# One pair deeper in the attention, and staged gate weights in the experts

## The chip, the cores and the metric

The kernel runs on one core of one Trainium2 chip. TensorE (PE) multiplies matrices, VectorE (DVE) and ScalarE (ACT) work element by element, GpSimd (Pool) does here mainly indirect transfers (gather and scatter of rows), and SyncE (SP) issues the other transfers. They run in parallel and wait for one another through semaphores. The metric is the device time of one execution in microseconds.

## The reference

Two layers over 16 sequences of 256 tokens with 128 features. Layer 0 is a recurrent mixer gated by an 8-expert network; the change doesn't touch it. Layer 1 is an attention of 16 heads gated by a network of 160 experts, of which each token uses 8:

```python
q = proj(wq, bq); k = proj(wk, bk); v = proj(wv, bv)          # 16 heads of 64
scores = jnp.einsum('bhqd,bhkd->bhqk', q, k) * scale
attn = jax.nn.softmax(scores, axis=-1)
ctx = jnp.einsum('bhqk,bhkd->bhqd', attn, v)
s = jnp.einsum('bsd,hd->bsh', ctx, wo) + bo
...
combine = combine.at[jnp.arange(T)[:, None], top_idx].set(top_w)   # 8 of 160 experts
h1 = jax.nn.silu(jnp.einsum('th,eih->eti', x, w_gate))             # 64 hidden each
routed = jnp.einsum('eti,ehi->th', h1 * combine.T[:, :, None], w_down)
shared = jax.nn.silu(x @ w_gate_shared.T) @ w_down_shared.T
x = x + s * silu(routed + shared)
```

## The kernel before, in words

Layer 1 comes in three stages: the attention of sequences 0 to 7, then the experts, then the attention of sequences 8 to 15. Beside the first half Pool scatters the tokens to the experts' slots in DRAM (`xs_dram`, 256 scatters of 128 rows, L555), and DVE works out the routing weights. Beside the second half Pool gathers the experts' rows (L567, 256 gathers), and DVE adds them up, weighted.

**The attention** goes by pairs of heads, 8 for each sequence, 64 for a half, numbered p. The steps of a pair are a chain over the engines: PE projects q and k (`qk_mm`, three passes each, high and low parts), ACT writes the high part and DVE the low part (`qk_out`, `qk_low`); PE makes the scores of both heads (`both_scores`, L1045) in `ps_s`, DVE takes the negated row maxima (L1734), ACT the exponentials with their sums (`exps`, L741, two for each head); PE turns the probabilities (`turn_probs`, L1058), ACT copies them (`probs_out`, L718), PE multiplies them with the values (`values`, L1078). Beside that DVE inverts and spreads the sums (`invert_sums`, `spread_sums`, L1699), PE turns them (`turn_rsums`, L1066), ACT copies them (`rsums_out`, L733), DVE normalises the context (`normalise`, L1706) and PE projects it (`project`, L1088). Each engine runs a fixed order written by hand, in which different steps belong to different pairs. A step that finds its semaphore too low stops all that stands behind it on its engine. For the scores of pair p, `attend` on PE waits until the exponentials of pair p-1 have read the banks (`exp_done`).

Pool's scatters are paced: every second one waits for `tr_done`, the count of turned heads, so that they spread over the half; each also waits until an earlier one has landed.

**The experts** run over 42 iterations (`NBODY`) of 1024 slots, in two halves h of four tiles of 128 slots. A tile belongs to one pair of experts (2 x 64 hidden columns make 128), whose number stands in a table (`pair_row`). For a half, PE turns the slots (`turn_slots`), ACT copies them (`xT_out`); PE multiplies them with the gate weights (`up1`): the slots are the stationary operand and the weights, at an address that PE reads from the table, are streamed. ACT applies SiLU (`silu`), PE turns the result (`turn_hidden`), DVE writes it masked by which expert of the pair owns the slot (`hidden_out`; `own_of` makes the mask), PE multiplies with the down weights (`down_1`), ACT or DVE copies the rows, and SP stores them. Pool has nothing to do in this stage.

## Time and profile before

| | |
|---|---|
| median of 3 runs | 1999.31 us (1998.68 to 2007.2) |
| the profiled execution's own time | 1999.14 us |
| its span | 1997.3 us |
| busy: PE, DVE, ACT, Pool | 1750.2, 1208.2, 971.0, 687.6 us |
| first half of the attention | 853.5 to 1282.1 us |
| experts | 1282.1 to 1512.5 us |
| shared expert | 1512.5 to 1547 us |
| second half of the attention | 1547 to 1995 us |

Times of the profile count from the start of the span. The stages' edges were set by hand: the first scores of each half, the first slots that PE turns (1282.10), and the shared expert's start. Names of tiles that share memory can stand for one another: `xn_buf` holds maxima and sums of the attention, and the slots and, in the changed kernel, the staged weights of the experts; `gate` is the gate weights.

### The profile page before, as it was taken

What the parts mean: (1) busy time and instruction counts of PE and PEld (TensorE: products, weight loads), DVE (VectorE), ACT (ScalarE), POOL (GpSimd) and SP (SyncE); (2) the same over time, 40 slices, a digit from 0 to 9 for tenths busy, and PEclk for the clock granted to TensorE, in tenths of its full rate; (3) what the DMA queues carried; (4) which work ended last, traced back from release to release, by engine and by line L of the source; (5) the groups of instructions that cost most, each with busy time, mean ns of one, the idle gap of its engine ahead of it and who ended that gap; (6) DMA issues with size and microseconds to landing.
All of it is one profiled execution on the core that took longest, in us unless ns stands there. A gap on an engine that the chain in (4) does not pass through costs nothing.

```text
span 1997.3 us, 47676 instructions
## 1 busy us (share of the span) xinstructions
PE 1750.2 (88%) x13222; PEld 1445.1 (72%) x13309; DVE 1208.2 (60%) x4593; ACT 971.0 (49%) x3034; POOL 687.6 (34%) x735
## 2 busy tenths in 40 slices
PE   5889999999999996787888888899997888777878
PEld 2557699999999776465666666699995666565656
DVE  4553445555555677866666766666663666666667
ACT  2311244444444224365666666655552666555656
POOL 0034412222222004255555555300003555555552
PEclk9988999999999998798999999999998899999999
DMA  9901101111110302111111111377672111111111
GB/s 355 373 21 34 35 24 37 37 37 37 37 37 26 87 0 99 78 34 42 65 39 66 41 64 39 111 197 197 197 198 74 36 45 38 41 42 42 44 42 30
DMA packets 153598, 153.77 MB, mean 77 GB/s; under 512 B 17027, under 2 KB 132294, under 8 KB 153286
## 3 DMA queue, kind: packets, MB, share of 16 engines
q1 hardware_dynamic: 130404, 104.23, 16.5%
q0 software_dynamic: 22272, 47.29, 7.8%
q10 hardware_dynamic: 866, 1.58, 0.2%
q8 instruction: 25, 0.41, 0.1%
q14 instruction: 31, 0.25, 0.0%
HBM read 71.10 MB, written 81.94 MB: 77 GB/s over the span
## 4 chain that ended last, share of the span: by engine, by line
PE 60%; DVE 14%; another core or an unknown queue 9%; issue 8%; ACT 7%; DVEq 1%; DMA 1%; ACTq 0%
PE ps_y L861 7%; ACT probs L741 5%; PE ps_up L1045 4%; PE ps_y L919 4%; PE ps_up L910 4%; PE ps_up L1140 4%; PE ps_t L1157 4%; PE ps_y L1058 3%; PE ps_rec L874 3%; PE ps_rec L876 3%; PE ps_t L879 3%; PE ps_t L877 3%; PE ps_rec L1015 3%; DVE xn_buf L1734 3%
## 5 line engine op out<-in xcount | busy, mean ns | idle before, releaser
L567 POOL DMA_INDIRECT rows_g<-ys_dram,slot x256 | 248.7, 971 | 446.7 <-DMA ys_dram<-slots_y 241.7
L741 ACT ACTIVATE probs<-ps_up,xn_buf 128x256 f32<-128x256 f32 x512 | 236.4, 477 | 191.0 <-DVE xn_buf L1734 166.1
L555 POOL DMA_INDIRECT xs_dram<-xn_buf,slot x256 | 247.3, 966 | 198.3 <-issue 89.8
L1734 DVE TENSOR_REDUCE xn_buf<-ps_up 128x2 f32<-128x512 f32 x256 | 166.9, 687 | 208.9 <-remote 123.6
L1058 PE MATMUL ps_y<-misc,probs 128*128 128x128 f32 x1024 | 171.6, 298 | 115.6 <-ACT probs L741 92.2
L1058 PEld LDWEIGHTS ps_y<-misc,probs 128*128 128x128 f32 x1024 | 117.2, 148 | 161.6 <-ACT probs L741 135.0
L861 PE MATMUL ps_y<-zeros 128*128 128x512 bf16 x660 | 193.8, 388 | 1.8 <-issue 0.2
L1354 DVE SCALAR_TENSOR_TENSOR mixn<-ps_rec,cols_sb,th_r 128x16 f32<-128x16 f32 x256 | 59.8, 233 | 217.7 <-ACT th_r L625 116.9
L525 POOL DMA_INDIRECT ys_dram<-slots_y,row_ids x80 | 78.1, 977 | 300.9 <-DVE slots_y L1484 240.3
L718 ACT COPY probsT<-ps_y 128x512 f32<-128x512 f32 x256 | 147.8, 598 | 32.9 <-remote 16.4
L1078 PE MATMUL ps_t<-probsT,v_sb 128*64 128x256 f32 x1024 | 143.1, 400 | 5.9 <-ACT probsT L718 3.3
L625 ACT ACTIVATE th_r<-ps_rec 128x16 f32<-128x16 f32 x256 | 46.7, 182 | 208.2 <-PE ps_rec L874 196.6
L1045 PE MATMUL ps_up<-kT,qT 64*128 64x256 f32 x1536 | 136.8, 314 | 0.3 <-issue 0.3
L1015 PE MATMUL ps_rec<-xr,w_high 128*128 128x256 f32 x528 | 123.8, 329 | 4.9 <-DVE xr L1669 3.5
L865 PEld LDWEIGHTS ps_rec<-gin,misc 128*128 128x128 f32 x514 | 98.5, 193 | 40.1 <-issue 6.9
L1045 PEld LDWEIGHTS ps_up<-kT,qT 64*128 64x128 f32 x1536 | 109.4, 203 | 19.7 <-issue 5.5
L1088 PE MATMUL ps_t<-aw,ctxT 128*128 128x128 f32 x512 | 94.6, 309 | 25.4 <-DVE ctxT L1706 16.6
L919 PE MATMUL ps_y<-w_sb,h_sb 128*128 128x128 f32 x640 | 110.5, 295 | 0.0
L644 ACT ACTIVATE h_sb<-ps_up,b_sb 128x256 f32<-128x256 f32 x160 | 75.9, 474 | 69.6 <-PE ps_y L919 63.3
L868 PEld LDWEIGHTS ps_t<-gin,misc 128*128 128x128 f32 x514 | 88.0, 193 | 28.9 <-issue 15.6
L910 PE MATMUL ps_up<-slots_xT,w_sb 128*128 128x256 f32 x320 | 108.5, 421 | 0.0
L627 ACT ACTIVATE th_zv<-ps_t 128x32 f32<-128x32 f32 x256 | 50.6, 198 | 116.7 <-PE ps_t L879 108.5
(250 smaller groups left out, 4364.6 us busy)
## 6 DMA issues: line engine op xcount, KB each, us to landing
xn_buf<-xs_dram SPq DMA_DIRECT2D x88, 256.0 KB, 2.8
xs_dram<-zeros SPq DMA_DIRECT2D x42, 512.0 KB, 5.7
ys_dram<-slots_y SPq DMA_DIRECT2D x84, 256.0 KB, 2.4
slots_x<-xs_dram SPq DMA_DIRECT2D x41, 130.0 KB
xs_dram<-zeros SPq DMA_DIRECT2D x10, 520.0 KB, 4.6
gate<-w_gate SPq DMA_DIRECT2D x1, 5120.0 KB, 15.9
down<-w_down SPq DMA_DIRECT2D x8, 640.0 KB
w_sb<-w POOLq DMA_DIRECT2D x16, 256.0 KB, 3.0
```

The lines of the kernel that those rows point to most:

```text
L555: nc.gpsimd.indirect_dma_start(xs_dram, bass.IndirectOffsetOnAxis(ap=slot[:, n, k:k + 1], axis=0), xn_tok[:, n, :], None).then_inc(scatter ...
L567: nc.gpsimd.indirect_dma_start(rows_g[:, i % 16, :], None, ys_dram, bass.IndirectOffsetOnAxis(ap=slot[:, i // TOPK1, i % TOPK1:i % TOPK1 + ...
L718: nc.scalar.copy(probsT[:, a, :, :].rearrange("p c t -> p (c t)"), ps_y[:, a, :]) \
L741: nc.scalar.activation(probs[:, a, i, :], ps_s[a][:, T * i:T * i + T], ACT.Exp, bias=negmax[:, a, i:i + 1], accum_out=sums[:, j % 4, i, a: ...
L861: nc.tensor.matmul(ps_y[:, 1, :], warm_b[:, 0:P], warm_b[:, 0:512], start=True, stop=True)
L910: nc.tensor.matmul(ps_up[j % 2][:, 0:256], w1_sb[:, wbuf, P * j:P * j + P], slots0_xT[:, :], start=True, stop=True).then_inc(up_ready, 1)
L919: last = nc.tensor.matmul(ps_y[:, 0, P * s:P * s + P], h_sb[:, j % 2, P * s:P * s + P], w2_sb[:, wbuf, j, :], start=(j == 0 and s == 0), s ...
L1015: last = nc.tensor.matmul(dst, left[a_], right[b_], start=(k == 0), stop=(k == 2))
L1045: last = nc.tensor.matmul(ps_s[a][:, T * i:T * i + T], qT[rows_a, j % 2, a_, P * i:P * i + P], kT[rows_a, j % 2, b_, :], start=(k == 0), s ...
L1058: last = nc.tensor.transpose(ps_y[:, a, T * kc + P * i:T * kc + P * i + P], probs[:, a, i, P * kc:P * kc + P], ident)
L1078: last = nc.tensor.matmul(ps_ctx[HD * a:HD * a + HD, 0:T], v_sb[:, j % 2, kc, HD * a:HD * a + HD], probsT[:, a, kc, :], start=(kc == 0), s ...
L1734: V.tensor_reduce(negmax[:, a, :], ps_s[a][:, :].rearrange("p (i t) -> p i t", i=2), AX_X, ALU.max, negate=True).then_inc(max_ready, 1)
```

## The change

**In the attention** PE, ACT and DVE turn, copy, invert and multiply for a pair one step older than before. PE's order in a pair p was: scores(p), project(p-2), value projection(p+1), values(p-1), turned sums(p-1), turned probabilities(p), query/key projection(p+2). It is now: scores(p), turned probabilities(p-1), value projection(p), turned sums(p-2), values(p-2), project(p-3), query/key projection(p+2). The turned sums have moved from the bank of the context to that of the value projection. The drain behind each half has more steps. Pool's scatters wait for the same counts shifted by two, while the turning comes one pair later.

**In the experts** Pool copies the gate weights of each tile, addressed by the table, to a staging buffer of two iterations (`staged`), and PE holds them as the stationary operand and streams the turned slots. The product then comes out turned, `turn_hidden` and its buffer go, and DVE masks the hidden in place in SBUF.

```diff
+        staged = xn_tok[:, 16:32, :].rearrange("p (u h s) d -> p u h (s d)", u=2, h=2)
...
-                        pool.wait_ge(tr_done, (n * TOPK1 + k) // 2 - 3)
+                        pool.wait_ge(tr_done, (n * TOPK1 + k) // 2 - 1)
...
+            def stage(it, h, u, waits=True):
+
+                pool.reg_load(pool_word[h], words[0:1, bass.ds(it * 2 + h, 1)])
+                if waits:
+                    pool.wait_ge(up1_done[h], it - 1)
+                for s in range(4):
+                    nc.gpsimd.tensor_copy(staged[:, u, h, P * s:P * s + P],
+                                          gate1[:, bass.ds(pair_of(pool, pool_word[h], s) * P, P)]) \
+                        .then_inc(staged_by_pool[h], 1)
+
+            for k in range(2):
+                pool.wait_ge(scattered[k], 16 * NT * TOPK1 // 2)
+            pool.wait_ge(gate_loaded, 16)
+            pool.wait_ge(table_loaded, 32)
+            for u in range(2):
+                for h in range(2):
+                    stage(u, h, u, False)
+            with pool.Fori(1, NBODY // 2) as i:
+                for u in range(2):
+                    for h in range(2):
+                        stage(i * 2 + u, h, u)
...
-                nc.scalar.copy(rsumsT[:, :], ps_ctx[:, T:2 * T]).then_inc(rsumsT_ready, 1)
+                nc.scalar.copy(rsumsT[:, :], ps_v[:, T:2 * T]).then_inc(rsumsT_ready, 1)
...
+                    if not (first and j < 2):
+                        rsums_out(p - 2, not (first and j == 2))
                     if not early:
-                        rsums_out(p - 1, not (first and j == 1))
-                    probs_out(p, 0, not early)
-                    probs_out(p, 1, not early)
-                    if j == PAIRS - 2:
+                        for a in range(2):
+                            probs_out(p - 1, a, not (first and j == 1))
...
+                    if not early:
+                        for a in range(2):
+                            turn_probs(p * 2 - 2 + a, p - 1, a, not (first and j == 1))
+                    v_mm_(b, j, p, x)
                     if not (first and j < 2):
-                        project(p - 2, (j - 2) % PAIRS, None if first else b)
-                    v_mm_(b + (j + 1) // PAIRS, (j + 1) % PAIRS, p + 1, x)
-                    if not early:
-                        values(p - 1, (j - 1) % PAIRS, not (first and j == 1))
-                        turn_rsums(p - 1)
-                    for a in range(2):
-                        turn_probs(p * 2 + a, p, a, not early)
+                        turn_rsums(p - 2)
+                        values(p - 2, (j - 2) % PAIRS, not (first and j == 2))
+                    if not (first and j < 3):
+                        project(p - 3, (j - 3) % PAIRS, None if first else b)
                     qk_mm(b + (j + 2) // PAIRS, (j + 2) % PAIRS, p + 2, x)
...
-            def up1(it, h):
-
-                pairs = pairs_of(next_word[h])
+                pe.reg_load(pe_word[h], words[0:1, bass.ds(it * 2 + h, 1)])
+
+            def up1(i, u, h):
+
+                it = i * 2 + u
                 pe.wait_ge(xT_ready[h], it + 1)
+                pe.wait_ge(staged_by_pool[h], 4 * it + 4)
                 for s in range(4):
-                    last = nc.tensor.matmul(ps_up[h][:, P * s:P * s + P], slots_xT[:, h, P * s:P * s + P],
-                                            gate1[:, bass.ds(pairs[s] * P, P)], start=True, stop=True)
+                    last = nc.tensor.matmul(ps_up[h][:, P * s:P * s + P], staged[:, u, h, P * s:P * s + P],
+                                            slots_xT[:, h, P * s:P * s + P], start=True, stop=True)
                 last.then_inc(up1_done[h], 1)
...
-            def turn_hidden(it, h):
-
-                pe.wait_ge(silu1_done[h], it + 1)
-                for s in range(4):
-                    last = nc.tensor.transpose(ps_y[:, h, P * s:P * s + P], hid[:, h, P * s:P * s + P], ident)
-                last.then_inc(h_turned[h], 1)
...
-            def down_1(it, h, reg):
-
-                pairs = pairs_of(reg)
+            def down_1(it, h):
+
                 pe.wait_ge(hT_ready[h], it + 1)
                 pe.wait_ge(y_out[h], it + 1)
                 for s in range(4):
-                    last = nc.tensor.matmul(ps_t[h][:, P * s:P * s + P], hidT[:, h, P * s:P * s + P],
-                                            down1[:, :, :].rearrange("p k n -> p (k n)")[:, bass.ds(pairs[s] * P, P)],
-                                            start=True, stop=True)
+                    last = nc.tensor.matmul(ps_t[h][:, P * s:P * s + P], hid[:, h, P * s:P * s + P],
+                                            down1[:, :, :].rearrange("p k n -> p (k n)")
+                                            [:, bass.ds(pair_of(pe, pe_word[h], s) * P, P)], start=True, stop=True)
                 last.then_inc(down1_done[h], 1)
...
             def expert_turn(i, u, rest=True):
 
                 it = i * 2 + u
-                if rest:
-                    up1(it, 0)
-                if rest:
-                    turn_hidden(it - 1, 1)
-                turn_slots(i, u + 1, 0)
-                if rest:
-                    down_1(it - 1, 0, last_word[0])
-                load_word(it + 1, 0)
-                up1(it, 1)
-                turn_hidden(it, 0)
-                turn_slots(i, u + 1, 1)
-                if rest:
-                    down_1(it - 1, 1, last_word[1])
-                load_word(it + 1, 1)
+                for h in range(2):
+                    if rest:
+                        down_1(it - 1, h)
+                        load_word(it, h)
+                    up1(i, u, h)
+                    turn_slots(i, u + 1, h)
...
-                project(p - 2, PAIRS - 2, None)
+                for a in range(2):
+                    turn_probs(2 * p - 2 + a, p - 1, a, True)
+                pe.wait_ge(v_ready, p)
+                turn_rsums(p - 2)
+                values(p - 2, PAIRS - 2, True)
+                project(p - 3, PAIRS - 3, None)
+                pe.wait_ge(normed, p - 1)
+                turn_rsums(p - 1)
                 if x == 0:
                     pe.wait_ge(qk_ready, p + 1)
                     turn_slots(0, 0, 0)
                 values(p - 1, PAIRS - 1, True)
-                turn_rsums(p - 1)
-                if x == 0:
-                    pe.wait_ge(gate_loaded, 16)
-                    pe.wait_ge(table_loaded, 32)
-                    for h in range(2):
-                        pe.reg_load(next_word[h], words[0:1, h:h + 1])
-                    up1(0, 0)
+                project(p - 2, PAIRS - 2, None)
                 project(p - 1, PAIRS - 1, None)
...
-                    if not (first and j < 2):
-                        normalise(p - 2)
-                    values_out(p, j, x, not (first and j < 2))
-                    if j == 2 and not first:
+                    if not (first and j < 3):
+                        normalise(p - 3, not (first and j == 3))
+                    if not early:
+                        values_out(p - 1, (j - 1) % PAIRS, not (first and j < 3))
+                    if j == 3 and not first:
...
-                    invert_sums(p, j)
+                    if not early:
+                        invert_sums(p - 1, j + 3, not (first and j == 1))
                     side_work(b, j, x, (2, 3))
-                    spread_sums(p, not early)
+                    if not early:
+                        spread_sums(p - 1, not (first and j == 1))
...
-                dve.wait_ge(h_turned[h], it + 1)
+                dve.wait_ge(silu1_done[h], it + 1)
                 dve.wait_ge(own_ready[h], it + 1)
-                V.tensor_tensor(hidT[:, h, :], ps_y[:, h, :], own[:, h, :], ALU.mult).then_inc(hT_ready[h], 1)
+                V.tensor_tensor(hid[:, h, :], hid[:, h, :], own[:, h, :], ALU.mult).then_inc(hT_ready[h], 1)
```

On PE, one pair of the attention before, from its scores (L1045) to the query/key projection (L1015); L1058 turns probabilities, L1088 projects, L1036 projects values, L1078 is the values, L1066 turns sums:

```order
L1045 MATMUL ps_up<-kT,qT 128x256 x12
L1088 MATMUL ps_t<-aw,ctxT 128x128 x2
L1036 MATMUL ps_rec<-aw,xb 128x128 x2
L1078 MATMUL ps_t<-probsT,v_sb 64x256 x4
L1066 MATMUL ps_t<-misc,top 128x128 x2
L1058 MATMUL ps_y<-misc,probs 128x128 x8
L1015 MATMUL ps_rec<-xr,w_high 128x256 x2
L1015 MATMUL ps_rec<-xr,w_low 128x256
L1015 MATMUL ps_rec<-xr,w_high 128x256 x2
L1015 MATMUL ps_rec<-xr,w_low 128x256
```

and the same stretch in the changed kernel (L1082 scores, L1095 probabilities, L1073 value projection, L1103 sums, L1115 values, L1125 project, L1052 query/key):

```order
L1082 MATMUL ps_up<-kT,qT 128x256 x12
L1095 MATMUL ps_y<-misc,probs 128x128 x8
L1073 MATMUL ps_rec<-aw,xb 128x128 x2
L1103 MATMUL ps_rec<-misc,top 128x128 x2
L1115 MATMUL ps_t<-probsT,v_sb 64x256 x4
L1125 MATMUL ps_t<-aw,ctxT 128x128 x2
L1052 MATMUL ps_rec<-xr,w_high 128x256 x2
L1052 MATMUL ps_rec<-xr,w_low 128x256
L1052 MATMUL ps_rec<-xr,w_high 128x256 x2
L1052 MATMUL ps_rec<-xr,w_low 128x256
```

Turning the probabilities has moved from in front of the query/key projection to right behind the scores. On ACT and DVE the rows of a pair read the same in both kernels; what differs is the pair to which the copies, the reciprocals and the products belong.

On PE, half an iteration of the experts before: the up product with an address calculation (ISA) for each tile, the turned hidden (L1148), the turned slots (L1117), and the first down product:

```order
L1140 ISA
L1140 MATMUL ps_up<-gate,slots_xT 128x128
L1140 ISA
L1140 MATMUL ps_up<-gate,slots_xT 128x128
L1140 ISA
L1140 MATMUL ps_up<-gate,slots_xT 128x128
L1140 ISA
L1140 MATMUL ps_up<-gate,slots_xT 128x128
L1148 MATMUL ps_y<-misc,hid 128x128 x4
L1117 MATMUL ps_rec<-misc,xn_buf 128x128 x4
L1157 ISA
L1157 MATMUL ps_t<-down,hidT 128x128
```

The same in the changed kernel, with the down product first (L1177), the table's word, the up product (L1168; `xn_buf` is the staged weights) and the turned slots (L1153):

```order
L366 ISA
L1177 MATMUL ps_t<-down,hid 128x128
L366 ISA
L1177 MATMUL ps_t<-down,hid 128x128
L366 ISA
L1177 MATMUL ps_t<-down,hid 128x128
L366 ISA
L1177 MATMUL ps_t<-down,hid 128x128
L1160 ISA
L1160 TENSOR_LOAD pair_row
L1168 MATMUL ps_up<-slots_xT,xn_buf 128x128 x4
L1153 MATMUL ps_rec<-misc,xn_buf 128x128 x4
```

The turned hidden is gone and the up product has no addresses. These stand now on Pool, half an iteration, where before there was nothing:

```order
L571 TENSOR_LOAD pair_row
L366 ISA
L575 COPY xn_buf<-gate 128x128
L366 ISA
L575 COPY xn_buf<-gate 128x128
L366 ISA
L575 COPY xn_buf<-gate 128x128
L366 ISA
L575 COPY xn_buf<-gate 128x128
L571 ISA
```

Four copies, each with an address calculation, behind one load from the table.

## Rows read from the trace of the kernel before

**Rows 1.** The page: the chain that ended last, by engine.
```profile
PE 60%; DVE 14%; another core or an unknown queue 9%; issue 8%; ACT 7%; DVEq 1%; DMA 1%; ACTq 0%
```

**Rows 2.** Windows: us, busy us (instructions) by engine, clock, DMA share, GB/s.
```profile
853.50:1282.10 428.60, 359.70 (x2804) 276.25 (x2804) 293.55 (x1058) 265.71 (x847) 239.52 (x248) 0.94 0.15 51
1282.10:1512.50 230.40, 227.25 (x2040) 225.66 (x2038) 139.50 (x217) 126.98 (x215) 0.00 (x0) 1.00 0.69 195
...
1547.00:1995.00 448.00, 365.32 (x2817) 275.34 (x2816) 301.31 (x807) 272.76 (x857) 233.46 (x240) 0.94 0.15 40
```

**Rows 3.** Timeline of PE, a pair without waiting: start, us, instruction, [idle before, releaser].
```profile
1180.78 0.98 PE L1045 MATMUL ps_up<-kT,qT 64*128 64x256 f32 x12
...
1185.89 0.98 PE L1045 MATMUL ps_up<-kT,qT 64*128 64x256 f32 x12
```

**Rows 4.** Timeline of PE and DVE, a late pair.
```profile
1267.08 0.98 PE L1045 MATMUL ps_up<-kT,qT 64*128 64x256 f32 x12
...
1271.52 1.29 DVE L1734 TENSOR_REDUCE xn_buf<-ps_up 128x2 f32<-128x512 f32 x2 [4.06 <-remote]
...
1273.11 0.47 DVE L1676 SCALAR_TENSOR_TENSOR kT<-ps_rec,xn_buf,kT 128x256 fp32r<-128x256 f32 x1
...
1274.31 0.66 PE L1058 MATMUL ps_y<-misc,probs 128*128 128x128 f32 x4 [0.26 <-issue]
...
1275.61 0.98 PE L1045 MATMUL ps_up<-kT,qT 64*128 64x256 f32 x12
```

**Rows 5.** Waits, first half: engine waits for whom, us, times, longest.
```profile
DVE xn_buf L1734 <- remote: 57.9, 19, 4.8
...
ACT rsumsT L733 <- remote: 49.9, 33, 3.2
```

**Rows 6.** Timeline of PE: the first and last scores of the halves.
```profile
853.51 1.65 PE L1045 MATMUL ps_up<-kT,qT 64*128 64x256 f32 x12
...
1547.06 1.65 PE L1045 MATMUL ps_up<-kT,qT 64*128 64x256 f32 x12
...
1982.76 0.98 PE L1045 MATMUL ps_up<-kT,qT 64*128 64x256 f32 x12
```

**Rows 7.** Timeline of Pool, its last scatters.
```profile
1268.59 0.96 POOL L555 DMA_INDIRECT xs_dram<-xn_buf,slot  x1 [0.77 <-issue]
...
1271.58 0.96 POOL L555 DMA_INDIRECT xs_dram<-xn_buf,slot  x1 [0.76 <-DMA xs_dram<-xn_buf,slot]
1272.85 0.96 POOL L555 DMA_INDIRECT xs_dram<-xn_buf,slot  x1 [0.30 <-issue]
```

**Rows 8.** Timeline of PE's weight loads, one half iteration of the experts.
```profile
1401.66 0.97 PEld L1140 LDWEIGHTS ps_up<-gate,slots_xT 128*128 128x128 f32 x8
1402.56 0.47 PEld L1148 LDWEIGHTS ps_y<-misc,hid 128*128 128x128 f32 x4
1402.99 0.47 PEld L1117 LDWEIGHTS ps_rec<-misc,xn_buf 128*128 128x128 f32 x4
1403.43 0.97 PEld L1157 LDWEIGHTS ps_t<-down,hidT 128*128 128x128 f32 x8
1404.32 0.86 PEld L1140 LDWEIGHTS ps_up<-gate,slots_xT 128*128 128x128 f32 x7
```

**Rows 9.** Groups of Pool: busy us, mean ns, idle before.
```profile
L539 POOL TENSOR_TENSOR gin<-gin 128x512 f32<-128x512 f32 x8 | 10.2, 1272 | 106.1 <-DVE gin L1523 106.1
L513 POOL COPY row_ids<-slots_x 128x4 int32<-128x4 int32 x40 | 7.8, 195 | 3.8 <-DMA slots_x<-xs_dram 3.6
...
L496 POOL MEMSET hist_s<- 64x4112 f32 x1 | 3.5, 3520 | 52.5 <-DVE xn_buf L1296 52.5
```

**Rows 10.** Timeline of DVE and Pool at the end of layer 0.
```profile
766.74 1.23 DVE L1266 TENSOR_TENSOR xn_buf<-x_tok,ln_mean 128x1024 f32<-128x1024 f32 x1
766.75 2.34 POOL L541 TENSOR_TENSOR x_tok<-x_tok,gin 128x512 f32<-128x512 f32 x1
```

**Rows 11.** Groups, experts: the mask on DVE.
```profile
L1782 DVE TENSOR_TENSOR rows_g<-iota,edge 128x512 f32<-128x512 f32 x76 | 51.8, 682 | 0.0
```

59 lines of the change are left out of this document (35 added, 24 removed).

## The prediction

> **What bounds the kernel now.** I read the page's chain first. PE carries 60% of it and DVE 14%, and 9% is time for which the profile has no sender, "another core or an unknown queue" [rows 1]. So PE is the spine, but a tenth of the time it waits for something that no engine's work explains. Next the windows, one for each stage that the change touches [rows 2]: the first half of the attention (853.5 to 1282.1, 428.6 us), the experts (230.4 us) and the second half (448.0 us). In the two halves PE is busy for 359.7 and 365.3 us, at a mean granted clock of 0.94; in the experts for 227.3 of 230.4 us at 1.00. The halves are bound by a loop of waits, the experts by PE itself.
>
> The pair loop. A half has 64 pairs. When nothing is late, one pair takes 5.11 us from scores to scores (1180.78 to 1185.89) with PE never idle [rows 3]. The mean is 428.6/64 = 6.70 us in the first half and 448.0/64 = 7.0 us in the second (the drain is in both). A late pair shows the loop [rows 4]: the scores start at 1267.08 and are done at 1268.06, DVE's maxima start only at 1271.52 (idle 4.06 us, released by "remote"), after the exponentials PE can turn the second half of the probabilities at 1274.31, and the next scores start at 1275.61. From the start of the maxima to the next scores that is 4.09 us. Since turning the probabilities stands in front of the next query/key projection on PE, every lateness of the maxima goes into the pair in full.
>
> How much is late: in the first half DVE's maxima wait 57.9 us for "remote", 19 times and up to 4.8 us, and ACT's copy of the turned sums 49.9 us [rows 5]. I do not know the cause; I take these arrivals as given and expect them to stay.
>
> **The change, attention.** No instruction is added or removed in a pair. Turning the probabilities of pair p, its copies, its values and its reciprocals come one pair later, the output projection too, and on ACT and DVE the rows read the same and only belong to an older pair. What waits for the exponentials of pair p is now scores(p+1), which overwrite the same banks. Count again from the start M of the maxima with the durations of [rows 4]. By the exponentials: PE started the step that follows the last of them at 1274.31, so the scores may start at M+2.8. By the other side: DVE finishes the low part of kT at 1273.58, M+2.06; then the projection for pair p+2 may start, which took 1.3 us less the 0.4 us of the transposes in front of it, so about 0.9 us, and the scores follow at M+3.1. So the loop is 3.1 us instead of 4.09 after M: 1.0 us less. With M at 1.2 us after the start of the scores the loop is 4.3 us plus lateness, against PE's 5.1 us; lateness up to 0.8 us costs nothing.
>
> What a pair can save is thus the smaller of 1.0 us and its distance to 5.1 us. I took the starts of the scores of all pairs, 64 from 853.51 to 1275.61 and 64 from 1547.06 to 1982.76 [rows 4, 6], and added that smaller number over the 63 intervals: 46 us in the first half (31 intervals are above 6.1 us, the others between), 56 us in the second (48 above). The bounds are nothing (the lateness moves along with the order) and the whole distance, 422.1 - 63 x 5.1 = 101 us and 435.7 - 321.3 = 114 us (all hidden, and the clock never dropped). I take 46 and 56, the edge that the loop sets. ACT's copies of the probabilities of p-2 must now be done before PE turns those of p-1 right behind the scores; that leaves about a microsecond, since ACT has 5.1 us for 265.7/64 = 4.2 us of work. DVE has 293.6/64 = 4.6 us of work in a pair, 4.7 in the second half [rows 2]: it fits under 5.1 us but is the next to be late.
>
> Each half drains one pair deeper. Behind the loop PE turns the probabilities of pair 63, then waits for the normalised pair 62 before it turns the sums of 63. I charge 4 us a half; between 0 and one whole pair, 6.7 us.
>
> A floor in the first half. Pool scatters four token blocks in each pair, and two of them take 3.0 us when Pool never waits (1268.59 to 1271.58) [rows 7]: 1.5 us each, 6.0 us a pair. The diff lets the first paced block go only in pair 2, at about 866; the 248 left take 372 us, to 1238 at the earliest. Before, the last one started at 1272.85, and the first slots were turned at 1282.1, where my window ends. With the same 9.3 us behind it the experts start at least 1272.85 - 1238, or 35 us, earlier at best. So the 46 - 4 = 42 us are cut; I write 36 us, since the delay behind the last scatter may shrink a little. Second half: 56 - 4 = 52, and I write 50.
>
> **The change, experts.** One iteration of 1024 slots has two halves of 2.66 us, with loads of the stationary operand back to back [rows 8]: up 0.90, turning the hidden 0.43, turning the slots 0.44, down 0.89. With the gate weights stationary the product comes out as the transpose that down needs, and the 0.43 us goes: 2.23 us, or 4.46 instead of 5.32 us for an iteration, 36 us over 42. ACT is busy for 127.0/42 = 3.0 us of an iteration and DVE for 139.5/42 = 3.3 us [rows 2], and neither gets an instruction more: both fit. DVE's product is now made before the next turn of PE needs it, with most of an iteration to spare. The slots' transfers had 0.69 of the DMA engines over this stage [rows 2]; at 4.46 us it would be 0.82: still under one.
>
> New is Pool: eight copies of 128 x 128 for each iteration, which no row shows. A copy of 4 columns took 0.195 us, and a two-input instruction of 512 columns 1.27 us, 2.5 ns a column [rows 9]. So a copy lies between 0.195 us and 0.195 + 124 x 2.5 ns = 0.50 us; the row that writes one operand and reads none, 4112 columns in 3.52 us, has 0.86 ns a column, which makes 0.30 us. I take 0.32 us and a gap of 0.07 us: 8 x 0.39 = 3.1 us.
>
> That would fit if Pool were alone. But DVE and Pool get in each other's way [rows 10]: at 766.74 DVE started a product of two SBUF operands (1.23 us) and Pool's instruction of the shape that takes 1.27 us alone [rows 9], 0.01 us later, took 2.34 us: 1.12 us of it came after DVE's end. So while one moves data the other stands; only about 0.15 us at an instruction's head runs beside. DVE has four such instructions an iteration in the changed kernel: two masks (0.68 us, [rows 11]), as before, and now the masked hidden, which used to read PSUM. Each stops Pool for up to 0.53 us; part of the 0.22 us between Pool's moves is covered, so I take 0.4 us each, 1.6 us. Pool then needs 3.1 + 1.6 = 4.7 us, a little more than PE. With the register loads (two an iteration) hidden under the copies I take 4.75 us: (5.32 - 4.75) x 42 = 24 us saved. Bounds: 4.46 us (36 saved) and 8 x 0.57 + 4 x 0.69 = 7.3 us (84 lost), where nothing overlaps and every copy is dear.
> The Trainium skill (SBUF — State Buffer, section "Who interferes with whom") says that a DVE instruction with two SBUF inputs and a GpSimd instruction that reads SBUF exclude each other, and the one that comes second waits for all of the first. The trace agrees (2.34 against 1.27 us); by that rule Pool waits, and the stage comes out at Pool's pace rather than at PE's 4.46 us.
> [...]
>
> **The sum.** 36 + 50 + 24 = 110 us less; all else (the recurrent layer before 853.5, the shared expert, the first pairs' start) is the same code. The profiled execution took 1999.1 us (span 1997.3), the median is 1999.3, so I predict 1889 us.
>
> **The rivals.**
> A, the forecast: the pair loop absorbs about 1 us of lateness, and the experts run near 4.75 us. 0.50.
> B, Pool binds the experts. For it: eight copies and four exclusions in 4.46 us are more than I can fit with certainty, and the copy's price is guessed. Against it: the head of each instruction runs beside the other engine's, and only the masks and products stop Pool. At 5.9 us an iteration the stage is 24 us longer instead of shorter: 1999 - 86 + 24 = 1937 us. 0.15.
> C, more than the loop's 1.0 us is won. PE idles less, so the granted clock of the halves goes from 0.94 towards 1.00, and pairs queue behind each other with a pair in hand. First half at its floor (-36 us), second at 5.6 us a pair (-90), experts at PE's pace (-36): 1837 us. 0.12.
> D, the attention gains nothing, since lateness only moves to a wait one step on (ACT's copies behind the scores, DVE's order): +8 us for the drains, -24: 1983 us; with half of the attention's gain it would be 1999 - 43 - 24 = 1932. 0.13.
> E, slower: the late arrivals come with Pool's transfers (of the late maxima in [rows 4] the release, 1271.52, lies 0.06 us before Pool's next scatter at 1271.58 [rows 7]). A faster loop keeps Pool busy in every pair, so that every pair is late, not every third. The loop is then 4.3 us plus lateness: with a mean lateness of 2.9 us it is 7.2 us, (7.2 - 6.85) x 128 = 45 us more, 8 for the drains, 24 less: 2028 us. It decides from 2.7 us of mean lateness (7.0 us a pair) upwards; the present mean is 57.9 + 49.9 over 64 pairs, 1.7 us. 0.10.
>
> **Numbers.** Predicted 1889 us. The likeliest case alone spans 1865 to 1915 us. The range of eight in ten takes in C's centre less a little and most of B and D: 1832 to 1965 us. Half a per cent, 10 us, is what a measurement of this kernel can tell from no change. Faster by more than that: A, B, C and nearly all of D, 0.87. Within it: the edge of D and E, 0.04. Slower: 0.09.
>
> **What would show it.** In the windows of the changed kernel: first half near 390 us, second near 398 us, experts near 200 us. In the pair loop PE's wait for the exponentials should stand at the scores and be less than half of now, with DVE's "remote" waits about as long. In the experts the interval from up to up should be 2.2 to 2.4 us, Pool's copies 0.32 us alone and 0.7 to 0.9 us when a mask is under way, and the waits of PE's up should name Pool's copies. The forecast is wrong if the pair stays at 6.7 us (D), if the "remote" waits grow (E), or if Pool is busy throughout and PE idles before up (B).

## The result and the profile after

The changed kernel took 2024.1 us (median of 4 runs, 2020.6 to 2028.0), the kernel before beside it 2000.3 us (4 runs, 1998.7 to 2007.2): ratio 1.0113, 95% interval 1.0082 to 1.0144. I had predicted 1889 us and a range of 1832 to 1965. The change made the kernel 1.1% slower, and the time lies far above the range. Throughout, a median and a ratio are of the runs at a kernel's own faster level, without those more than 1.5% above its fastest; the ratio is estimated from all of these runs, so it needn't be the quotient of the two medians, and its 95% interval stands in brackets.

The chain of work that ended last, which covered the whole span in [rows 1], can be followed back over two fifths of it now:

```profile
PE 19%; another core or an unknown queue 8%; DVE 4%; ACT 3%; issue 3%; DMA 1%; DVEq 0%; ACTq 0%; SPq 0%
```

Of what it covers, a fifth has no named sender. The windows say more: from the first to the last scores of each half, and between them from the first to the last up product of the experts. The columns are those of [rows 2]; the clock is the last number but two.

```profile
846.30:1268.30 422.00, 350.87 (x2733) 273.61 (x2733) 277.21 (x1038) 256.20 (x830) 237.17 (x244) 0.93 0.14 48
1285.50:1476.90 191.40, 191.21 (x1662) 187.79 (x1661) 142.73 (x210) 109.91 (x208) 157.56 (x320) 0.99 0.79 225
1514.50:2008.80 494.30, 383.74 (x2735) 295.93 (x2734) 292.46 (x784) 263.02 (x838) 231.60 (x240) 0.84 0.14 36
```

Before, the same stretch of the first half was 1275.61 - 853.51 = 422.1 us [rows 4, 6]: nothing won. The second half was 1982.76 - 1547.06 = 435.7 us [rows 6] and is 494.3 us: 58.6 us lost, at a granted clock of 0.84. The experts were 1285.2 to 1506.3, 221.1 us, and are 191.4 us: 29.7 us won. The first half starts 7 us earlier, which is no effect of the change: in the traces of e1 to e8, of both orders, it starts anywhere from 844.9 to 855.9. The drains (last scores to the experts' first up, and to the end) are 7.6 and 2.9 us longer, and the stretch between experts and second half is 3.2 us shorter: -7.2 - 0.1 + 7.6 - 29.7 - 3.2 + 58.6 + 2.9 = 28.9 us, the difference of the spans (2026.3 - 1997.3 = 29.0) but for rounding.

Two waits of the second half before (engine, whom it waits for, us, times, longest), and then four in the changed kernel:

```profile
POOL rows_g L567 <- PE ps_y L1058: 77.6, 34, 16.0
DVE xn_buf L1734 <- remote: 65.7, 27, 5.9
```
```profile
POOL rows_g L599 <- DVE xn_buf L1661: 203.2, 88, 14.3
DVE top L1715 <- remote: 90.8, 19, 7.0
ACT probs L773 <- remote: 73.1, 34, 4.1
ACT rsumsT L765 <- remote: 56.1, 17, 5.3
```

What waits for "remote", a release with no named sender, has grown: all such waits of the second half add up to 82.8 us before and 273.7 us now (they overlap, so this is no time of the kernel). And of the other engines' work Pool waits for DVE's sums alone; in the kernel before it also waited for PE's turned probabilities. Now one bad stretch, the timeline of all engines (start, us, instruction, [idle before, releaser]):

```profile
1652.64 1.05 POOL L599 DMA_INDIRECT rows_g<-ys_dram,slot  x1 [3.63 <-DVE xn_buf L1661]
1653.07 0.98 PE L1082 MATMUL ps_up<-kT,qT 64*128 64x256 f32 x12
...
1655.40 0.38 PE L1103 MATMUL ps_rec<-misc,top 128*128 128x128 f32 x2
1655.71 1.08 PE L1115 MATMUL ps_t<-probsT,v_sb 128*64 128x256 f32 x8
...
1657.87 0.28 PE L1052 MATMUL ps_rec<-xr,w_low 128*128 128x256 f32 x1
...
1658.99 0.94 POOL L599 DMA_INDIRECT rows_g<-ys_dram,slot  x1 [0.30 <-DVE xn_buf L1661]
...
1661.37 0.41 PE L1082 MATMUL ps_up<-kT,qT 64*128 64x256 f32 x2 [1.00 <-issue]
...
1661.48 0.94 POOL L599 DMA_INDIRECT rows_g<-ys_dram,slot  x1 [0.30 <-issue]
...
1663.53 0.58 PE L1082 MATMUL ps_up<-kT,qT 64*128 64x256 f32 x2 [1.75 <-issue]
1664.27 0.37 ACT L765 COPY rsumsT<-ps_rec 128x256 f32<-128x256 f32 x1 [4.71 <-remote]
1664.34 0.29 DVE L1715 COPY top<-xn_buf 128x256 f32<-128x256 f32 x1 [5.64 <-remote]
...
1664.73 0.42 DVE L1724 TENSOR_TENSOR ctxT<-ps_t,rsumsT 128x256 f32<-128x256 f32 x1
...
1668.32 1.05 POOL L599 DMA_INDIRECT rows_g<-ys_dram,slot  x1 [5.90 <-DVE xn_buf L1661]
```

This is where the "remote" releases come from. PE turned the sums at 1655.40. ACT, which only waits for that, starts its copy at 1664.27, and DVE, which waits for the same turn, at 1664.34. Over this time Pool sends eight gathers in a row, one each 1.25 us, from 1652.64 to 1662.42. The values of 1655.71 are used at 1664.73, 0.46 us after the sums, though they are 1.08 us of work for PE: as far as the recorded starts go, not the work was late but its signal, the rise of the semaphore that the others wait for. I call a row of Pool's transfers with at most 0.5 us between one and the next a train.

The trace also holds the moments at which semaphores rose, which the views don't print. By them the signal of these sums came at 1664.25 and that of the values at 1664.34; the turns that PE ended by 1655.1 were signalled at 1656.97 and 1658.46. PE itself stands still too: behind eight of its twelve scores it waits 1.00 us and then 1.75 us, for nothing that the profile names ("issue").

Then the clock:

```profile
1647.60:1659.00 11.40, 10.32 (x89) 8.10 (x88) 8.18 (x22) 6.22 (x21) 5.94 (x8) 1.00 0.13 35
1659.00:1663.50 4.50, 1.15 (x10) 1.01 (x11) 0.00 (x0) 0.56 (x4) 2.81 (x3) 0.99 0.22 58
1663.50:1671.70 8.20, 7.00 (x36) 5.14 (x35) 6.14 (x17) 5.76 (x17) 2.77 (x3) 0.59 0.06 16
```

PE was busy for 1.15 of 4.5 us, and the clock that follows is 0.59, a mixture of 1.2 and 2.4 GHz in which eight turns take 1.94 instead of 1.09 us. Over the whole stretch from first to last scores the kernel before had

```profile
1547.10:1982.80 435.70, 357.28 (x2757) 269.58 (x2756) 293.42 (x789) 267.60 (x842) 233.46 (x240) 0.94 0.16 41
```

PE is busy for 383.7 us in the changed kernel and was for 357.3 us here, with no instruction more. So 26 of the 58.6 us lost are work that took longer, beside a clock of 0.84 instead of 0.94, and 32 us are idle time of PE (110.6 against 78.4).

Counted over the second half, Pool's 240 gathers went in 14 trains of eight and 27 of four; before, 53 of four and one of seven. Where trains of eight come, they mostly come every three pairs, about 24 us apart.

### The profile page after: what moved, and what is told of

It is laid out like the page before. It is cut to its first block and busy times, and to the rows that moved or that the text cites. A ratio compares the mean times of both kernels' runs of the same rounds, so it can differ in the third digit from the quotient of the medians.

```text
span 2026.3 us, 47608 instructions
## 1 busy us (share of the span) xinstructions
PE 1744.1 (86%) x12878; PEld 1442.2 (71%) x12965; DVE 1202.5 (59%) x4593; ACT 950.6 (47%) x3034; POOL 849.0 (42%) x1072
## 5 line engine op out<-in xcount | busy, mean ns | idle before, releaser
L1082 PE MATMUL ps_up<-kT,qT 64*128 64x256 f32 x1536 | 151.0, 316 | 70.0 <-ACT probs L773 41.2
L1095 PE MATMUL ps_y<-misc,probs 128*128 128x128 f32 x1024 | 166.1, 314 | 49.1 <-ACT probsT L750 37.0
L1095 PEld LDWEIGHTS ps_y<-misc,probs 128*128 128x128 f32 x1024 | 130.8, 160 | 74.1 <-issue 58.9
L1082 PEld LDWEIGHTS ps_up<-kT,qT 64*128 64x128 f32 x1536 | 114.2, 202 | 94.9 <-ACT probs L773 44.2
L575 POOL COPY xn_buf<-gate 128x128 f32 x336 | 161.6, 523 | 33.1 <-PE ps_up L1168 30.6
L1052 PE MATMUL ps_rec<-xr,w_high 128*128 128x256 f32 x528 | 116.4, 313 | 63.5 <-DVE kT L1690 44.5
L750 ACT COPY probsT<-ps_y 128x512 f32<-128x512 f32 x256 | 139.7, 608 | 56.8 <-remote 30.9
L1115 PE MATMUL ps_t<-probsT,v_sb 128*64 128x256 f32 x1024 | 159.4, 429 | 3.1 <-issue 3.0
L1052 PEld LDWEIGHTS ps_rec<-xr,w_high 128*128 128x128 f32 x528 | 83.8, 198 | 76.3 <-DVE kT L1690 55.2
L1125 PEld LDWEIGHTS ps_t<-aw,ctxT 128*128 128x128 f32 x512 | 71.6, 202 | 56.5 <-issue 54.8
```

The costliest lines, as they stand in the source:

```text
L575: nc.gpsimd.tensor_copy(staged[:, u, h, P * s:P * s + P], gate1[:, bass.ds(pair_of(pool, pool_word[h], s) * P, P)]) \
L750: nc.scalar.copy(probsT[:, a, :, :].rearrange("p c t -> p (c t)"), ps_y[:, a, :]) \
L1052: last = nc.tensor.matmul(dst, left[a_], right[b_], start=(k == 0), stop=(k == 2))
L1082: last = nc.tensor.matmul(ps_s[a][:, T * i:T * i + T], qT[rows_a, j % 2, a_, P * i:P * i + P], kT[rows_a, j % 2, b_, :], start=(k == 0), s ...
L1095: last = nc.tensor.transpose(ps_y[:, a, T * kc + P * i:T * kc + P * i + P], probs[:, a, i, P * kc:P * kc + P], ident)
L1115: last = nc.tensor.matmul(ps_ctx[HD * a:HD * a + HD, 0:T], v_sb[:, j % 2, kc, HD * a:HD * a + HD], probsT[:, a, kc, :], start=(kc == 0), s ...
```

## The experiments

Six sets of runs, each beside the kernel before. In the first two (e1 to e4, e5 to e8) that kernel took 2002.7 and 2002.3 us. In the other four (e9 to e12, e13 to e16, e17, e18) it took 1838.3, 1843.9, 1842.3 and 1854.8 us, and no trace of theirs shows PE's signals late. So there are two kinds of session, and which one comes can't be chosen; the chip of e5 to e8 and that of e9 to e12 have the same number. No trace of the kernel before is kept from the second kind. "Half" below is the time from first to last scores, of the attention's first or second half.

**e1, the experts alone.** The kernel before with Pool's staging, up and down as in the change; the attention as before.


> The kernel before, with only the experts' part of the change (Pool stages the gate weights, no turn of the hidden); the attention's order is the old one. In the changed kernel an expert half iteration takes 2.30 us instead of 2.65. Theory P (the loss sits in the second attention half alone, and the experts gained): 84 x 0.35 = 29 us less than before, about 1970 us, ratio 0.985; second half still 436 us from first to last scores. Rival X (the staged experts harm what follows, for instance a colder start of the second half): second half above 445 us and 1980 us or more.


1970.8 us, ratio 0.983 (0.977 to 0.990). Halves 428.5 and 439.6 us, an expert half iteration 2.285 us, near what theory P expected. The experts' part is a gain by itself, and the loss is the attention's.

**e2, the gathers' threshold.**
```
-    pool.wait_ge(tr_done, 2 * HB * PAIRS - 2 + (i - 16) // 2)
+    pool.wait_ge(tr_done, 2 * HB * PAIRS + (i - 16) // 2)
```


> The changed kernel, but Pool's gathers wait for the turned probabilities with the old threshold (no -2), so that a gather may start one pair later at the earliest. Theory P (PE's completion signals are held up while Pool issues indirect transfers in a row; the -2 took the pacing by PE away and let Pool send eight in a row after DVE's sums): trains of eight vanish, the second half goes from 494 us (first to last scores) to 436 us or less, whole about 1960 to 1970 us. Rival L (the deeper order itself makes the second half slow, through DVE's later reciprocals and sums; the gathers only follow): second half stays at 480 to 500 us, whole 2015 to 2030 us.


1953.6 us, ratio 0.976 (0.970 to 0.981). Second half 416.4 us, clock 0.97, no train of eight. One number of the change cost the second half 494.3 - 416.4 = 78 us; with the old threshold the deeper order shortens it, by 435.7 - 416.4 = 19 us. Its window, from first to last scores, has PE busy for 344.0 us, so that 40 of the 78 us were work that took longer:

```profile
1511.50:1927.90 416.40, 343.95 (x2733) 263.78 (x2732) 291.73 (x784) 255.51 (x838) 233.24 (x240) 0.97 0.16 43
```

A regular pair of this kernel:

```profile
1787.40 0.94 POOL L599 DMA_INDIRECT rows_g<-ys_dram,slot  x1 [1.79 <-remote]
...
1789.62 0.98 PE L1082 MATMUL ps_up<-kT,qT 64*128 64x256 f32 x12
...
1791.28 0.95 POOL L599 DMA_INDIRECT rows_g<-ys_dram,slot  x1 [0.30 <-issue]
...
1793.15 1.29 DVE L1753 TENSOR_REDUCE xn_buf<-ps_up 128x2 f32<-128x512 f32 x2 [1.88 <-remote]
...
1793.97 0.94 POOL L599 DMA_INDIRECT rows_g<-ys_dram,slot  x1 [1.74 <-remote]
```

The scores of 1789.62 are used 0.92 us after the train's end (1792.23), and 0.8 us later the next train starts: 4.83 + 0.92 + 0.82 = 6.57 us. This pair is as long as four transfers and the way round from the train's end to the next train.

**e3 and e4, no gathers**, in the new and in the old order: 240 of the 256 gathers left out (`for i in range(16)`); the sums read what the first 16 brought.


> The changed kernel, with 240 of the 256 gathers of the second half left out (the sums read the rows that the first 16 brought). Theory P: without Pool's transfers nothing is late, a pair takes 4.95 to 5.2 us as the two pairs without transfers do, second half 315 to 330 us, whole about 1850 us. Rival L: the order is the cause, the second half stays above 440 us and the whole above 1970 us.

> The kernel before, with the same 240 gathers left out. Theory P: the loop of 4.09 us behind the maxima then has no lateness to add; a pair takes 5.1 to 5.4 us, second half 325 to 340 us instead of 436, whole about 1895 us. Rival R (the release that the profile does not name comes from elsewhere, and the gathers are innocent): second half 425 us or more, whole about 1990 us. The difference to the run without gathers in the new order says what the deeper order is worth by itself: under theory P 0 to 0.3 us a pair.


1847.7 us (0.922, 0.916 to 0.928) and 1882.0 us (0.940, 0.934 to 0.946). The windows of the second half, new and then old:

```profile
1516.30:1830.20 313.90, 312.37 (x2735) 250.83 (x2734) 285.11 (x784) 255.88 (x838) 0.00 (x0) 0.99 0.02 6
```
```profile
1553.40:1877.50 324.10, 321.63 (x2755) 252.95 (x2754) 289.62 (x788) 266.68 (x842) 0.00 (x0) 1.00 0.02 6
```

PE is busy throughout, and no wait for "remote" stands among the first eight of either stretch. A gather costs (435.7 - 324.1)/240 = 0.47 us in the old order, (494.3 - 313.9)/240 = 0.75 in the changed kernel and 0.43 in e2. Without them the deeper order is worth 324.1 - 313.9 = 10 us a half, 0.16 us a pair.

**e5, the loose threshold in the old order**: the -2 put into the kernel before.


> The kernel before (old order, old experts) with one edit: its gathers wait for the turned probabilities with the -2 of the changed kernel. Theory P (the lost pacing by PE is what cost 58 us, whatever the order): Pool follows DVE's sums alone, trains of eight appear, second half above 470 us instead of 436, whole about 2035 to 2060 us. Rival Q (only the deeper order, where PE's turns sit right behind the scores, falls into the pattern): second half within 5 us of 436, whole 1995 to 2010 us.


2004.9 us, ratio 1.0006 (0.998 to 1.004), second half 442.8 us, trains of four. My theory in its strong form falls: the -2 does harm only with the deeper order.

**e6, half of the rows**: e2 with `rows_g[0:64, ...]` for the 240 gathers.


> The changed kernel with the old gather threshold (1953.6 us), and each of the 240 paced gathers fetches 64 rows instead of 128 (the other 64 rows of the sum are left out). If Pool's issue and the hold on PE's signals go by the instruction: still 0.95 us each, second half 410 to 420 us, no change. If they go by the row: about 0.5 to 0.6 us each, a train of four takes 3.3 us instead of 4.8, a pair comes near PE's 5.1 us, second half 330 to 370 us, whole 1870 to 1910 us.


1947.9 us, ratio 0.970 (0.965 to 0.974); second half 413.4 us against 416.4. A gather of 64 rows takes 0.90 us of Pool (median), one of 128 took 0.94. The price is by the instruction, and half of the bytes bring nothing.

**e7, two under way**: e2, a gather waits for the landing of the one two before it.


> The changed kernel with the old gather threshold (1953.6 us), and a gather waits for the landing of the one two before it instead of three, so that gaps open inside a train of four. If a gap of half a microsecond lets PE's signals out: DVE's maxima start earlier in the pair, second half 385 to 410 us. If the pair is simply as long as Pool's four transfers and the way back to the next train: gaps make it longer, 420 to 450 us, whole 1957 to 1990 us.


1944.5 us, ratio 0.969 (0.965 to 0.973); second half 413.9 us, between the two expected ranges. The gathers go in trains of one and two, and far fewer of PE's signals are late (the count is below). Yet the half is no shorter than in e2: DVE's sums now wait 108.0 us for landings, and PE's value projection 67.3 us for DVE. Most signals were let out, and another wait took the place of theirs, so the run doesn't show what late signals alone cost.

**e8, no scatters**: the changed kernel without 248 of its 256 scatters, so that most tokens never reach the experts.


> The changed kernel, with 248 of the 256 scatters of the first half left out (tokens 128 and up are not sent to the experts; gathers as in the changed kernel). Theory P: the first half too is as long as it is because of Pool's transfers; without them 4.95 to 5.15 us a pair, 312 to 325 us instead of 422, whole about 1920 us. Rival R (the first half has another cause, such as DVE's 4.6 us of work): 390 us or more.


1917.0 us, ratio 0.957 (0.953 to 0.961).

```profile
846.00:1162.30 316.30, 312.66 (x2733) 251.98 (x2732) 274.13 (x1037) 255.05 (x830) 4.47 (x16) 0.98 0.05 17
```

So the first half too owes 106 us to Pool's transfers, while its second half stays at 491.2 us with 14 trains of eight. Pairs with exactly four scatters took 6.43 us in the kernel before (34 pairs) and 6.42 us in the changed one (27 pairs): the order made no difference under them.

**The signals counted.** For each step of PE that raises a semaphore, I take the time from the end of its work to the next rise of that semaphore. In the table are the steps with more than 0.3 us. Some rises are missing in the traces, which makes a signal look about a pair late, so a few of the counts are too high; a zero is safe.

| late signals of PE | first half | second half |
|---|---|---|
| before | 373 of 563 | 335 of 563 |
| changed | 404 of 558 | 319 of 558 |
| e2 | 400 of 558 | 389 of 558 |
| e3, no gathers, new order | 398 of 558 | 0 of 558 |
| e4, no gathers, old order | 346 of 563 | 0 of 563 |
| e7, two under way | 384 of 558 | 147 of 558 |
| e8, no scatters | 0 of 558 | 317 of 558 |
| e9 to e18 | 7 to 17 of 558 | 0 to 9 of 558 |

In the stretches with a zero the longest delay is 0.03 us. In the experts' stage no signal is late in any run, Pool's copies beside it or not: copies don't hold signals. Nor does a transfer that stands alone. In the kernel before, work of PE that ended during the first gather of a train was signalled 0.01 us later (median of 67), during the third 2.60 us later (71); and during the 80 indirect transfers of layer 0 (L525), which stand at least 2.5 us apart, it was 0.01 us (138). What holds signals is transfers in a row, from the second or third on; the scatters of the first half, with 0.30 and 0.77 us between them [rows 7], are such a row all through.

**e9 to e12**, in the second kind of session. e9 and e10 replace the gathers of e2 by plain transfers of 128 consecutive rows, issued by Pool (240 of them) or by SP (all); e11 and e12 have -1 and +2 in the threshold.


> The changed kernel with the old gather threshold (1953.6 us, second half 416 us), and 240 of the gathers replaced by plain transfers of 128 consecutive rows of the same size, still issued by Pool (so the sums get other rows). If any transfer that Pool issues holds up PE's signals: second half 400 to 430 us, whole 1940 to 1960 us. If it is the indirect form: the waits without a named releaser vanish, second half 315 to 335 us, whole about 1860 us.

> The same plain transfers, all 256, issued by SP's queue with the same waits; Pool does nothing in the second half. Theory P (Pool's issuing is the cause, not the bytes nor the landing): second half 314 to 330 us as without gathers, whole 1850 to 1870 us. Rival T (the traffic into SBUF or its landing signals hold PE up): second half above 380 us.

> The changed kernel with -1 instead of -2 in the gathers' threshold. Of each four gathers the first two are then released by PE's turn of the same pair and the last two by DVE's sums, as all four are with -2. If it is DVE's sums as the trigger that let trains of eight form: they are back, at least some, second half 450 to 495 us, whole 1985 to 2025 us. If a threshold one step higher is enough for the pacing: 415 to 425 us, whole 1950 to 1960 us.

> The changed kernel with +2: all four gathers of a pair are released by PE's signals right behind the scores, and DVE's sums are never the last. If a pair in this regime is Pool's train of four (4.8 us), the 0.9 us until PE's signals come and the 0.7 us until the next train: 6.4 us, second half 400 to 416 us, whole 1937 to 1955 us, no better than +0. If more slack helps to hide the train: under 395 us.


1806.3, 1799.9, 1818.4 and 1808.7 us beside 1838.3: ratios 0.988 (0.972 to 1.004), 0.979 (0.969 to 0.988), 0.989 (0.983 to 0.995) and 0.984 (0.974 to 0.994). All halves took 314 to 320 us, although the gathers of e12 went in trains of up to 85. In this kind of session Pool holds nothing up, so none of the four tells what it was made for, not even where a time falls near one of the expected ones.

**e13, the changed kernel again; e14 to e17**, e9, e10 and twice e11 again.


> The changed kernel unaltered, as control. In a session like the first two (before at 2000 us): 2015 to 2030 us, second half about 494 us. In one like the last (before at 1831 to 1850 us, no late signals): the experts' 29 us and some us of the second half are gained, the first half waits for Pool's last scatter in both kernels, so about 35 us less than before, 1800 to 1815 us.


e13: 1808.6 us beside 1843.9, ratio 0.983 (0.966 to 0.999), as expected for this kind. Here the change is a gain, though it barely clears its interval. One of its pairs:

```profile
1700.31 0.95 POOL L599 DMA_INDIRECT rows_g<-ys_dram,slot  x1 [0.49 <-DVE xn_buf L1661]
...
1700.49 0.98 PE L1082 MATMUL ps_up<-kT,qT 64*128 64x256 f32 x12
...
1701.56 0.95 POOL L599 DMA_INDIRECT rows_g<-ys_dram,slot  x1 [0.30 <-DMA rows_g<-ys_dram,slot]
...
1702.02 1.28 DVE L1753 TENSOR_REDUCE xn_buf<-ps_up 128x2 f32<-128x512 f32 x2
...
1705.45 0.39 PE L1082 MATMUL ps_up<-kT,qT 64*128 64x256 f32 x2
```

Pool sends one transfer each 1.25 us all through, DVE goes on to the maxima without waiting, and the pair takes 4.96 us. What ends the first half here is Pool (the windows from first to last scores and from there to the experts, and PE's first work for them):

```profile
828.60:1143.70 315.10, 311.44 (x2733) 251.12 (x2732) 275.47 (x1037) 254.95 (x830) 181.90 (x188) 0.99 0.15 53
1143.70:1246.00 102.30, 13.27 (x93) 9.27 (x93) 7.69 (x27) 8.28 (x22) 62.23 (x77) 0.57 0.18 61
```
```profile
1240.26 1.09 PE L1153 MATMUL ps_rec<-misc,xn_buf 128*128 128x128 f32 x4 [87.14 <-DMA xn_buf<-xs_dram]
```

The expectations of e14 to e17 gave the alternatives of e9 to e11 for a session of the first kind; for one of the second those of e14, e15 and e17 gave 1800 to 1803 us. It was the second; e14 to e16 took 1805.6, 1802.1 and 1804.6 us, ratios 0.979 (0.963 to 0.995), 0.976 (0.959 to 0.992) and 0.976 (0.963 to 0.988), e17 alone 1804.8 us beside 1842.3 and 0.980 (0.969 to 0.990).

**e18, four scatters under way**, on top of e2:
```
-                    if n or k >= 2:
-                        pool.wait_ge(scattered[k % 2], 16 * (n * (TOPK1 // 2) + k // 2))
+                    if n or k >= 4:
+                        pool.wait_ge(scattered[k % 4], 16 * (n * 2 + k // 4 + (NT if k % 4 > 1 else 0)))
```
(the other two semaphores are those of layer 0, which stand at 16 NT; the waits for the last scatters are changed to match)


> The changed kernel with the gathers' threshold at +0 and up to four scatters under way instead of two. In a session without late signals (before at 1830 to 1870 us): Pool needs 1.25 us a scatter instead of 1.5, four a pair fit into 5.0 us, the last is out soon after the last pair, so the experts start near 1160 instead of 1246 us and the whole takes 1710 to 1730 us. If something else held the scatters (the landing itself, the pacing by PE's turns), 1780 to 1800 us. In a session with late signals (before at 2000 us): trains of four in the first half too, as in the second, 410 to 425 us for the half, whole 1940 to 1960 us.


1730.3 us beside 1854.8, ratio 0.9385 (0.931 to 0.946), at the upper edge of the expected range. Pool's last scatters and its first copies:

```profile
1162.19 0.96 POOL L564 DMA_INDIRECT xs_dram<-xn_buf,slot  x1 [0.30 <-issue]
1163.46 0.96 POOL L564 DMA_INDIRECT xs_dram<-xn_buf,slot  x1 [0.30 <-issue]
1166.71 4.41 POOL L575 COPY xn_buf<-gate 128x128 f32 x16 [2.30 <-issue]
```

The last scatter starts at 1163.5 instead of 1235.1 and the experts at 1175 instead of 1246 us. It beats both kernels in this kind of session; in the other kind e2 does (0.976), and e18 was not measured there.

## Why the prediction was wrong

**The step that failed** is "I take these arrivals as given and expect them to stay", the foundation of the 46 and 56 us. The late arrivals were neither given nor foreign: they are PE's own signals, held back while Pool sends transfers in a row (e3, e4, e8 and the count of the signals). A pair with four transfers then lasts as long as the transfers and the way round (6.57 us in e2), and shortening PE's loop behind the maxima by 1.0 us saves little or nothing. The first half took 422.0 us, against 422.1 before and a forecast saving of 36; the second half saved 19 us even in e2, against 56 forecast for the loop. Once no signals are late, PE is busy all through in the old order too, and the deeper one is worth 10 us in the second half (e3, e4).

**Second half, -50 forecast, +58.6 measured.** The prediction follows the scatters' threshold and never speaks of the gathers' -2, which the lines of the diff shown ahead of it don't have either. In the kernel before PE turned the second half of the probabilities 1.3 us ahead of the next scores [rows 4]; in the changed one it does so 1.4 us behind their start (median), 2.7 us later. The -2 takes back a whole pair, 6.7 us, where 2.7 were due: PE's turns stopped pacing, and Pool followed DVE's sums. That the -2 cost the 78 us in this order is shown (e2). That trains of eight follow from it only when PE has the next scores ready inside a train, as the deeper order has, fits e5 (no harm in the old order) and the timeline above, where signals come through between the first transfers and DVE's sums of 1656.86 to 1658.7 feed Pool again. This part is argued, not shown: e11, which was to test it, never met such a session.

**Rival E** had the cause of the late arrivals (chance 0.10, 2028 us; measured 2024.1). Its price was close by luck: it spread 45 us over both halves by a lateness in every pair, and what came were 58.6 us in one half, in every third pair or so, 26 of them in PE's work, longer at a lower clock; and no faster loop brought it, but the threshold. Its row was there: the release of 1271.52 beside Pool's scatter of 1271.58 [rows 4, 7]. A count over the starts of the scores and of Pool's transfers would have shown it: the two pairs of the second half without a Pool transfer took 5.3 us, those with four 7.0.

**Experts, -24 forecast, -29.7 measured.** The size is near, but the term had the wrong engine as the limit: it put Pool a little above PE, at 4.75 us an iteration, with PE's up waiting for the copies. The interval from up to up was forecast at 2.2 to 2.4 us and is 2.30 (before 2.66 [rows 8]), 4.59 us an iteration; PE is busy for 191.2 of 191.4 us, and it is Pool that waits for PE's up, 30.6 us. Pool's copies:

```profile
L575 POOL COPY xn_buf<-gate x336: 288/295/822, 1277.6 to 1469.4; 128x128 f32 x168
```
```profile
L575 POOL COPY xn_buf<-gate 128x128 f32 x336 | 161.6, 523 | 33.1 <-PE ps_up L1168 30.6 <-issue 2.1
```

Minimum, median and maximum are 0.288, 0.295 and 0.822 us, where I had 0.32 alone and 0.7 to 0.9 behind a mask. 177 of the 336 copies take 0.30 us or less and the other 159 take 0.745 or more, each beside a DVE instruction with two SBUF inputs, about four of the eight of an iteration: the four exclusions that the prediction counted. What it had too much is the gap of 0.07 us between copies. They follow without one, and Pool is busy for 161.6/42 = 3.8 us an iteration in 4.59. PE binds, at 0.13 us an iteration more than the 4.46 that I had for it, and Pool fits: rival B is refuted.

**The drains**, 4 us each forecast, were 7.6 and 2.9 us.

**The floor in the first half**, Pool's last scatter at 1238 at the earliest. That Pool sets this limit is right, and e13 shows it where the loop is fast enough to reach it: PE waited 87 us for what follows the last scatter. That it started there at 1235.1, so near to 1238, is luck. The first half of e13 starts 25 us earlier than the one that I counted from, and its scatters took 1.59 us each (from 841.2 on), not 1.5. I had written that two take 3.0 us "when Pool never waits", while the row has 0.76 us of waiting for an earlier landing [rows 7]; that wait is the limit of two under way. I did not ask what a loop at 5.0 us would be worth if the limit were moved: with four under way, in e18, a scatter takes 1.31 us and the experts start 71 us earlier than in e13.

**In the other kind of session** the forecast fails too, in another way. In the changed kernel the loop's late arrivals were not there. If they were not there in the kernel before either, of which no trace is kept, the order could save only the 0.16 us a pair of e3 and e4, and the first half ends with Pool's scatters whatever the order; what is left is the experts' 30 us, which fits the measured 0.983.

The Trainium skill (SBUF — State Buffer, section "SBUF: two separate sides") says that TensorE's port never waits on anyone. This case's traces don't contradict it for the data, since the matmuls were issued, but a reader who takes from it that PE is safe from Pool errs: the signal of work that ended at 1655.78 by the profile rose at 1664.25, 8.5 us later, and PE itself stood twice in the middle of its scores. The measurement decides.

**What stays open.** Why a session is of one kind or the other. Whether only indirect transfers hold signals or any that Pool issues in a row (e9, e14 met no session that could tell), or the traffic rather than the issuing (e10, e15; half the bytes changed nothing in e6). What between PE and its semaphores is held. How far the clock and the held signals can be told apart: PE's longer work is 26 of the 58.6 us, but the two come together in every trace of the changed kernel. Whether e18 is a gain where signals are late.

## What to carry to other kernels

A wait with no named releaser is not weather: count it against what every other engine does, here against trains of transfers issued by Pool, before it goes into a forecast as a constant. When a schedule is shifted, each threshold that counts its events has to be shifted by the time that the event moved, not by its index; here the -2, a whole pair for an event that moved by 2.7 us, cost the second half 78 us. And one session's verdict on such a change can have the other sign in the next: run before and after side by side more than once.

## What the runs showed of the hardware

- In some sessions PE's signals are held back while Pool issues indirect transfers in a row: those of work started from 1654.9 to 1657.9 came after 1663.5, behind eight transfers. Work that ends during the first gather of a train is signalled at once (0.01 us), during the third 2.60 us later (medians of the kernel before). The next signal after a train of four rises 1.0 us after its last transfer (median of 53 trains); behind the train of eight shown above the bulk came 1.8 us after it. Pool's copies hold nothing: no late signal in the experts' stage. In other sessions the same kernel has 4.96 us a pair under unbroken trains.
- The price of a gather is by the instruction: 0.90 us of Pool for 64 rows, 0.94 us for 128, and the same second half.
- A stretch in which PE was busy for 1.15 of 4.5 us was followed by a granted clock of 0.59; a second half with 14 trains of eight had 0.84, against 0.94 in the kernel before, 0.97 in e2 and 0.99 without gathers.
- With a wait for the landing of the one two before, two scatters take 3.0 us (1268.59 to 1271.58 [rows 7]); with four under way they follow 1.27 us apart (1162.19, 1163.46).
- Copies of 128 x 128 on Pool take 0.295 us, and 0.745 to 0.822 us when a DVE instruction with two SBUF inputs is under way.
- DVE's mask of 512 columns takes 0.77 us beside Pool's copies; it took 0.68 [rows 11].
